# The last stage of a graph network: residual sum by accumulating transposes, deeper buffers, later steps

## The reference, cut to what matters

```python
alpha = ex / (denom[dst] + 1e-16)                    # softmax over the edges of one node, 4 heads
agg = segment_sum(vj * alpha[:, :, None], dst)       # 128 channels a node
out = agg.reshape(n, HID) + (x @ Wskip + bskip)
h = gelu(gelu(out @ W1 + b1) @ W2 + b2)
x = layernorm(x + (out + h))                         # no scale, no shift
```

## Time and profile before

| | |
|---|---|
| time, median of 3 runs (lowest, highest) | 7416.07 us (7416.06, 7416.97) |
| span of the profiled execution | 7463.9 us |
| busy in the span: TensorE, VectorE, GpSimd, ScalarE | 6262.2, 6114.0, 4840.9, 3838.3 us |
| last stage: first block's transpose to last scatter | 6651.07 to 7456.24 us |

### The profile page before, as it was taken

How to read it: one execution, slowest core, us unless ns; L and a number is a source line. 1 busy time by engine, 2 the same in 40 slices (tenths; PEclk the granted TensorE clock), 3 DMA queues, 4 the chain that set the end, 5 groups by cost and what they waited for, 6 DMA issues and landing times. The chain is left out here.

```text
span 7463.9 us, 156875 instructions
## 1 busy us (share of the span) xinstructions
PE 6262.2 (84%) x37260; PEld 5197.7 (70%) x37260; DVE 6114.0 (82%) x15796; ACT 3838.3 (51%) x10696; POOL 4840.9 (65%) x5469
## 2 busy tenths in 40 slices
PE   7699889899999657989989998999888765877776
PEld 3588888888889436867766676667666554865664
DVE  8588778787888777889879977997799887878887
ACT  6466666666666576733661166116622233654443
POOL 0488888888873576855776577657744565546665
PEclk8799999999999899999999999999999998988998
DMA  0365555554444466879779977997799765543432
GB/s 2 102 165 161 161 160 158 162 161 152 146 145 152 146 190 199 247 257 297 229 223 332 329 226 224 331 327 228 230 385 387 259 186 151 152 138 119 125 123 86
DMA packets 981268, 1483.74 MB, mean 199 GB/s; under 512 B 156967, under 2 KB 450705, under 8 KB 980647
## 3 DMA queue, kind: packets, MB, share of 16 engines
q1 hardware_dynamic: 685479, 922.39, 37.2%
q0 software_dynamic: 141504, 309.42, 16.2%
q10 hardware_dynamic: 153664, 244.12, 9.0%
HBM read 902.58 MB, written 573.11 MB: 198 GB/s over the span
## 5 line engine op out<-in xcount | busy, mean ns | idle before, releaser
L1336 PE MATMUL bank<-c_rows,sums_all 128*128 128x256 f32 (+1 forms) x3920 | 1320.9, 420 | 550.5 <-DVE c_rows L1487 304.3
L751 PE MATMUL bank<-wf_w,c_xt 128*128 128x256 f32 x6272 | 1615.0, 381 | 2.0 <-DVE y L1545 2.0
L1381 ACT ACTIVATE c_xt<-bank 128x512 f32<-128x512 f32 (+1 forms) x980 | 556.8, 568 | 1586.6 <-issue 831.0
L1307 POOL DMA_INDIRECT c_rows<-t_tab,src_pair x784 | 870.2, 1110 | 705.6 <-PE bank L1336 546.2
L1336 PEld LDWEIGHTS bank<-c_rows,sums_all 128*128 128x128 f32 x3920 | 633.9, 194 | 984.7 <-DVE c_rows L1487 478.7
L751 PEld LDWEIGHTS bank<-wf_w,c_xt 128*128 128x128 f32 x6272 | 1133.7, 191 | 127.0 <-ACT c_xt L1381 3.5
L1487 DVE SCALAR_TENSOR_TENSOR c_rows<-bank,carry,c_rows 32x256 f32<-32x256 f32 (+1 forms) x1950 | 913.7, 469 | 274.3 <-PE bank L1336 117.6
L1307 POOL DMA_INDIRECT c_rows<-z_tab,src_pair x784 | 770.7, 983 | 293.3 <-issue 189.5
L1085 DVE TENSOR_TENSOR lx_lo<-bank,lx_hi 128x512 fp32r<-128x512 f32 (+1 forms) x1000 | 658.6, 659 | 260.6 <-ACT lx_hi L1030 217.4
L1030 ACT ACTIVATE lx_hi<-bank 128x512 fp32r<-128x512 f32 (+1 forms) x1000 | 569.4, 572 | 580.4 <-PE bank L999 418.6
L741 PE MATMUL bank<-wf_hi,lx_hi 128*128 128x256 f32 x3200 | 725.0, 309 | 62.7 <-issue 49.4
(11 more groups left out here) (333 smaller groups left out, 14629.2 us busy)
## 6 DMA issues: line engine op xcount, KB each, us to landing
c_z<-z_tab SPq DMA_DIRECT2D x882, 256.0 KB
z_tab<-lz SPq DMA_DIRECT2D x400, 256.0 KB
t_tab<-lt SPq DMA_DIRECT2D x400, 256.0 KB
z_tab<-y ACTq DMA_DIRECT2D x392, 256.0 KB
c_own<-z_tab SPq DMA_DIRECT2D x392, 256.0 KB
t_tab<-y ACTq DMA_DIRECT2D x392, 256.0 KB
c_own<-t_tab SPq DMA_DIRECT2D x392, 256.0 KB
fl_x<-x_tab SPq DMA_DIRECT2D x396, 128.0 KB
```

Source lines behind the costliest of these rows:

```text
L751: last = nc.tensor.matmul(out, x(k), w[:, k, :], start=(k == 0), stop=(k == ks - 1 and not bias))
L1307: pool.indirect_dma_start(out=rows[:, s, i, 0:win], out_offset=None, in_=source, in_offset=bass.IndirectOffsetOnAxis(ap=m["src_i"][:, t:t ...
L1336: nc.tensor.matmul(psum[s % 2][:, i * win:(i + 1) * win], sums[:, j * 2 + i, :], rows[:, s, i, 0:win], start=True, stop=True).then_inc(S[" ...
L1381: nc.scalar.activation(xt[:, s % 2].rearrange("p k n -> p (k n)")[:, 0:n], psum[2 + s % 2][:, 0:n], ACT.Copy).then_inc(S["copied"], 1)
```

## The change

The second load of x and VectorE's two additions go. `back` no longer transposes one finished sum: it transposes `xt`, `skip` and `down` of a half block one after the other into the same PSUM bank, accumulating (six transposes a block where there were two). ScalarE copies the result to `y` (`result`), where VectorE had written it. The `agg` product with the identity is marked as a transpose. `xt`, `skip` and `y` get 6 slots, the statistics 8, and the scatters count on a ring of 6. `back` runs 4 turns after its block's first (before 5), the moments 5 (6), `scale_both` 8 (7), `scatter_both` 9 (7). `divide` and `norm` are cut into single steps that are interleaved in VectorE's list.

```diff
-                            "down_set": 1, "sum": 1, "back": 1, ...
+    out_ring = counts.phase(finish, {"scattered*": 32}, ring=6)
-        x_again = sb("fl_x2", [P, 4, 2, D])
-        xt = sb("fl_xt", [P, 2, 2 * P])
-        skip = sb("fl_skip", [P, 4, 2 * P])
+        xt = sb("fl_xt", [P, 6, 2 * P])
+        skip = sb("fl_skip", [P, 6, 2 * P])
-        both = sb("fl_sum", [P, 2, 2 * P])
-        y = sb("fl_y", [P, 4, 2, D])
+        y = sb("fl_y", [P, 6, 2, D])
# SyncE
-                                 (BEGIN - 4, every, load), (5, each, far_again)])
+                                 (BEGIN - 4, every, load)])
# GpSimd
-                in_turns(total, [(7, each, scatter_both), (6, each, invert)])
+                in_turns(total, [(9, each, scatter_both), (6, each, invert)])
# TensorE
                         for i in range(2):
                             last = nc.tensor.matmul(psum[3][:, i * P:(i + 1) * P], agg[:, c % 4, i, :], ident[:],
-                                                    start=False, stop=(i == 1))
+                                                    start=False, stop=(i == 1), is_transpose=True)
                 def back(j):
-                    pe.wait_ge(S["sum"], fp.at("sum", j))
+                    pe.wait_ge(S["down_set"], fp.at("down_set", j))
                     if j >= 2:
                         pe.wait_ge(S["y"], fp.at("y", j - 2))
                     for i in range(2):
-                        last = nc.tensor.transpose(psum[6 + j % 2][:, i * P:(i + 1) * P],
-                                                   both[:, j % 2, i * P:(i + 1) * P], ident[:])
+                        half_ = psum[6 + j % 2][:, i * P:(i + 1) * P]
+                        terms = (xt[:, j % 6, :], skip[:, j % 6, :], down[:, j % 2, :])
+                        for n, term in enumerate(terms):
+                            last = nc.tensor.matmul(half_, term[:, i * P:(i + 1) * P], ident[:], start=(n == 0),
+                                                    stop=(n == 2), is_transpose=True)
-                                 (BEGIN + 3, every, add_up(1)), (2, each, up_), (3, each, down_), (5, each, back)])
+                                 (BEGIN + 3, every, add_up(1)), (2, each, up_), (3, each, down_), (4, each, back)])
# ScalarE
+                def result(j):
+                    act.wait_ge(S["back"], fp.at("back", j))
+                    if j >= 6:
+                        act.wait_ge(S[f"scattered{j % 6}"], out_ring.ring_at("scattered", j, j % 6, back=1))
+                    nc.scalar.activation(y[:, j % 6, :, :].rearrange("p i c -> p (i c)"), psum[6 + j % 2][:, 0:2 * P],
+                                         ACT.Copy).then_inc(S["y"], 1)
-                in_turns(total, [(0, each, copy), (1, 1, line_copy), ...
+                in_turns(total, [(5, each, result), (0, each, copy), (1, 1, line_copy), ...
# VectorE
-                                 (BEGIN + 2, every, carry_on(0)), (7, each, scale_both),
-                                 (BEGIN + 5, every, divide), (6, each, norm), (BEGIN + 3, every, carry_on(1)),
-                                 (4, each, add), (BEGIN + 1, every, weigh)])
+                                 (BEGIN + 2, every, carry_on(0)), (BEGIN + 5, every, denominators),
+                                 (5, each, moments), (BEGIN + 5, every, inverses), (5, each, aggregate),
+                                 (BEGIN + 5, every, of_leads), (8, each, scale_both), (5, each, variance),
+                                 (BEGIN + 3, every, carry_on(1)), (BEGIN + 5, every, divide),
+                                 (BEGIN + 1, every, weigh)])
```

More of the change, by code:

```diff
@@ L124, in ring_at @@
         rate = self.rate[name + "*"]
-        return (j - s) * (rate // self.ring) + (self.base.get(name + str(s), 0) + rate * (1 - back))
+        before = (j - s) // self.ring * rate if isinstance(j, int) else (j - s) * (rate // self.ring)
+        return before + (self.base.get(name + str(s), 0) + rate * (1 - back))
     def end(self, name):
@@ L2174, in down_ @@
                     if j >= 2:
-                        act.wait_ge(S["sum"], fp.at("sum", j - 2))
+                        act.wait_ge(S["back"], fp.at("back", j - 2))
                     nc.scalar.activation(down[:, j % 2, :], psum[5][:, 0:2 * P], ACT.Gelu_apprx_tanh,
                                          bias=m["b_down"][:]).then_inc(S["down_set"], 1)
-                in_turns(total, [(0, each, copy), (1, 1, line_copy), (1, each, skip_), (2, each, up_), (3, each, down_),
+                def result(j):
+                    act.wait_ge(S["back"], fp.at("back", j))
+                    if j >= 6:
+                        act.wait_ge(S[f"scattered{j % 6}"], out_ring.ring_at("scattered", j, j % 6, back=1))
+                    nc.scalar.activation(y[:, j % 6, :, :].rearrange("p i c -> p (i c)"), psum[6 + j % 2][:, 0:2 * P],
+                                         ACT.Copy).then_inc(S["y"], 1)
+                in_turns(total, [(5, each, result), (0, each, copy), (1, 1, line_copy), (1, each, skip_), (2, each, up_), (3, each, down_),
                                  (18, 1, weight)])
@@ L2299, in carry_on, with denominators, inverses, of_leads @@
                     return step
[L2301 removed]
+                def denominators(j):
                     s = j % 4
                     dve.wait_ge(S["summed"], ph.at("summed", j))
[L2304 to L2305 removed]
                     bank = psum[s % 2][:, 0:2 * wide].rearrange("p (i n) -> p i n", i=2)
                     v.tensor_scalar(den[:, s, :, :], bank[:, :, D:wide], DEN_EPS, None, ALU.add).then_inc(S["den"], 1)
+                def inverses(j):
+                    s = j % 4
                     dve.wait_ge(S["den"], ph.at("den", j, 1))
                     v.reciprocal(den[:, s, :, :], den[:, s, :, :]).then_inc(S["den"], 1)
+                def of_leads(j):
+                    s = j % 4
                     dve.wait_ge(S["den"], ph.at("den", j, 2))
@@ L2313, in divide @@
                                     ALU.mult).then_inc(S["den"], 1)
+                def divide(j):
+                    s = j % 4
+                    if j >= 4:
+                        dve.wait_ge(S["skip"], fp.at("skip", order.index(j - 4)))
+                    bank = psum[s % 2][:, 0:2 * wide].rearrange("p (i n) -> p i n", i=2)
                     dve.wait_ge(S["den"], ph.at("den", j, 3))
@@ L2319, in divide, with moments, aggregate @@
                     last.then_inc(S["shared"], 1)
[L2321 to L2324, removed]
-                    v.tensor_tensor(both[:, j % 2, :], skip[:, j % 4, :], down[:, j % 2, :], ALU.add
-                                    ).then_inc(S["sum"], 1)
-                def norm(j):
-                    s = j % 4
-                    dve.wait_ge(S["back"], fp.at("back", j))
-                    dve.wait_ge(S[f"others_in{s}"], fp.ring_at("others_in", j, s))
-                    if j >= 4:
-                        dve.wait_ge(S[f"scattered{s}"], fp.ring_at("scattered", j, s, back=1))
-                    v.tensor_tensor(y[:, s, :, :].rearrange("p i c -> p (i c)"), psum[6 + s % 2][:, 0:2 * P],
-                                    x_again[:, s, :, :].rearrange("p i c -> p (i c)"), ALU.add).then_inc(S["y"], 1)
+                def moments(j):
+                    s = j % 8
                     dve.wait_ge(S["y"], fp.at("y", j))
                     for i in range(2):
-                        last = v.bn_stats(stats[:, s, i, :], y[:, s, i, :])
+                        last = v.bn_stats(stats[:, s, i, :], y[:, j % 6, i, :])
                     last.then_inc(S["stats"], 1)
+                def aggregate(j):
+                    s = j % 8
                     dve.wait_ge(S["stats"], fp.at("stats", j, 1))
```

53 lines of the change are left out of this document (24 added, 29 removed).

## The result

The kernel after the change took 7437.79 us (median; 7430.23 to 7444.59) beside 7417.19 for the kernel before in the same sessions (7411.68 to 7424.34). The ratio is 1.0027, with an interval of 1.0019 to 1.0034: 20.6 us or 0.27% slower. The forecast was 7421, with a range of 7365 to 7455, so the time lies inside the range, and 17 us above the forecast. The direction was given as even between faster and the same, with slower the least likely of the three; the change is slower by a little more than the 0.2% that can be told from nothing.

What follows compares the result with a forecast made beforehand. Bound before: power, scale, scatter at 7.40 us a round; after: a ring through TensorE at 7.34. Terms -5 + 34 - 5 - 13 - 6 + 0 = +5 on 7416 gave 7421 us, range 7365 to 7455.

Steps and rivals of the forecast that it cites:

- the slots: `result` waits for the scatter of six blocks earlier: 4.96 + landing L, 6.5 us, under 7.34, so no cost.
- the head: Last stage up to its first `carry_on(1)`: GpSimd's two turns go from 7.4 to 6.3 us; -6 us, bounds 0 and -9.
- the part with one block a round: 19 rounds after the steady part, forecast to go from 5.74 to 5.0 us each: -13 us.
- the ring through TensorE: Steady part: `add_up(1)`, `back`, `result`, moments, scaling, `carry_on(1)` become the bound at 7.34 us a round, 7.2 to 7.9.
- Full-clock rounds: The 78 steady rounds at full clock go from 7.40 to 7.34 us each: -5 us.
- The clock's falls: Steady part: TensorE's drops to 1.2 GHz now cost 1.7 us each; 20 taken, +34 us, bounds 0 and 58.
- the clock stays up: Rival: TensorE's stop of 2.0 us is too short for a clock drop, total 7387 us; chance 0.20.
- the single long rounds: 8.5 us of few long steady rounds; those from GpSimd meet 1.1 us of slack: -5 us.
- Drain: Last four pairs of blocks, where power and scatter still follow each other at 7.40 us: change 0.
- GpSimd's ring: Rival: GpSimd's own work bounds the steady part at 6.28 us a round, total 7310 us; chance 0.11.
- Scaling stretches the scatters: Rival: VectorE's scaling keeps GpSimd from writing descriptors, GpSimd needs 7.40 us a round, total 7397 us; chance 0.08.
- Slower: the falls all come: Rival: 34 clock drops in the longer ring, or a landing of 2.8 us, total 7445 us; chance 0.16.

Runs made afterwards that it cites:

- scale_even: Kernel after with `scale_both` at start 7 instead of 8, so it falls in even turns of the steady part: 7333.94 us, ratio 0.9884.
- warm_filler: Kernel after with three matmuls a round, result never read, on TensorE ahead of `add_up(1)`: 7404.91 us, ratio 0.9978.
- y_eight: Kernel after with 8 slots of `y` and scatters counted on a ring of 8, `xt` and `skip` with 5 slots: 7414.44 us, ratio 0.9994.
- before_decoupled: Kernel before with `scatter_both` at start 9 instead of 7, `y` with 6 slots, statistics with 8: 7368.95 us, ratio 0.9936.

## Why the prediction came out as it did

The time came out within the range, at +20.6 where +5 had been added up. The ring that bounds the kernel and the price of a fall were right. The step that failed is the one on the slots, and the terms of the head and of the part with one block a round were too favourable.

**The bound: right.** "the ring through TensorE becomes the bound at almost the old period, and GpSimd's 6.28 stays unused" is what the chain of after shows, and `scale_even` shows that what holds GpSimd's 6.28 back is the scaling in that ring. Its terms were forecast at 4.44 + 0.04 + 0.38 + 0.04 + 2.02 + 0.42 = 7.34. The chain has 0.42 for carry to `add_up(1)`, 4.42 for TensorE (6990.19 to 6994.61), 0.44 for `result` with its handovers, and 1.96 from the moments to the carry (6995.05 to 6997.01): 7.24. The moments to the carry had been put at 2.02. The accumulating transposes cost what the passes of `agg` in the earlier trace rows had said: six starts between 6951.56 and 6952.11, 0.11 apart. VectorE's short steps hid where they were said to hide.

```profile
6951.56 0.27 PE L2127 MATMUL bank<-ident,fl_xt 128*128 128x128 f32 x1
6951.68 0.27 PE L2127 MATMUL bank<-ident,fl_skip 128*128 128x128 f32 x1
6951.78 0.27 PE L2127 MATMUL bank<-ident,fl_down 128*128 128x128 f32 x1
...
6952.11 0.27 PE L2127 MATMUL bank<-ident,fl_down 128*128 128x128 f32 x1
```

**Full-clock rounds:** forecast 78 x (7.34 - 7.40) = -5, measured 78 x (7.24 - 7.40) = -12.5. The ring was 0.10 shorter than its sum.

**The clock's falls:** the mechanism and the price were right (1.67 each, forecast 1.7), the number was 25, not 20, and so +42 instead of +34. The kernel before had 33 rounds with a fall, where the prediction had worked out some 34. The open question was whether a stop of 2.0 still lets the clock fall: it does, in 16 of the 67 rounds that have such a stop. The other 9 falls come behind stops of 2.24 to 3.40, which late landings made and which the prediction did not have. So 20 was nearer to the truth than it looks, partly by luck: it was a choice between 0 and 34, and no row had told it. The rival "the clock stays up" gave 7387, and `warm_filler`, whose clock did stay up, has 7405: 33 to 35 us less than after and not the 40 of 24 falls fewer, because the stray rounds grew by 5. The prediction also says that it needs more than 29 falls to be slower by over 0.2%; its own sum reaches +15 with 26 (+5, and 6 falls more at 1.7).

**The slots, and the single long rounds:** this is the step that failed. The prediction has "6.5, under 7.34, so it costs nothing" for the slots and "Of the 8.5 us, those from GpSimd now meet 1.1 us of slack: -5" for the long rounds. Those of GpSimd went (`y_eight` has none between 7.3 and 8.7), and others came in their place, 9.6 us over 7.24, so +1 instead of -5. They come from the slots, for the landing L, counted from the end of the issue, was taken as one number, 1.57, from a gather's consumer in the earlier trace rows. The threshold was right: 4.96 + L against 7.24 decides from L = 2.3 on. But L is a distribution. Its median is 1.2, even shorter than assumed; `result` waits 17 times in 78 rounds, and in the round at 6997.01 L is up to 3.8. `y_eight` takes the wait away, and the stray rounds and eight falls with it: the term was worth 23 us by the medians and had been put at 0.

**One block a round:** forecast -13 (its own product, 19 x (5.0 - 5.74), is -14), measured -7.4. The rounds alternate between 5.05 and 5.29 (forecast 5.0), which is 3 of the 6.7 missing. The first two take 6.99 and 6.18, and one further on 5.96. These three, and no other of the 19, have a granted clock of 0.71 to 0.76: falls, which the prediction had not put into this part. They are the rest.

**Head:** forecast -6, measured +0.9. From the second power on GpSimd takes 10.9, 8.7, 7.7, 6.9, 6.5 and 6.2 from one power to the next, so its ring of 6.3 is reached only where the head ends. The first power comes 24.9 us into the head, before 22.6. Beside VectorE's long scans over the running maximum a scatter takes longer:

```profile
6633.02 1.85 DVE L2251 TENSOR_TENSOR_SCAN r_up_to<-r_starts,r_side,r_al 128x784 f32<-128x784 f32 x1
6633.21 2.52 POOL L2031 DMA_INDIRECT out_dram<-fl_y,node_of  x1 [2.98 <-DVE fl_y L2362]
```

The head before had that too (its power beside the same scan took 2.52), so this alone doesn't explain the miss. The slots cost here as well: `result` waits 8.2 us for landings in the head, in 5 waits, and `y_eight` has a head of 75.4, 3.0 less. How the rest of the 7 us divides was not tried.

**Drain:** forecast 0, measured +0.2.

The sum of the terms is then -12.5 + 42 + 1 - 7.4 + 0.9 + 0.2 = +24.2 on the profiled execution, +20.6 by the medians. Against the forecast of +5 the stray rounds are off by 6, the head by 7, the part with one block by 6, the falls by 8, and the ring by -7.5 on the other side. The landing stands behind three of these at once, the stray rounds, the falls and a part of the head, and without it the change would have been neutral. That the total was only 17 us off is in part luck, for the ring's error ran the other way.

**The rivals.** GpSimd's ring (7310, given 0.11) did not come by itself and came with one digit changed. "Scaling stretches the scatters" (0.08) is refuted for this kernel: in `scale_even` the scatter beside the scaling took 0.97 and the scaling 1.21 instead of 1.12. The Trainium skill (SBUF — State Buffer, section "SBUF: two separate sides") says that VectorE in a two-port mode, or with two SBUF inputs against a GpSimd operation that reads SBUF, and GpSimd exclude each other for a whole instruction. In which mode the scaling ran no run here shows; the trace shows no such lock for it, and agrees with the rule beside the scan, which has two tensor inputs, where the scatter took 2.52. "Slower: the falls all come" had the side right and the cause half: 25 falls and not 34, with the landing added. It also said that a landing of 2.8 would do as much, for every round; it took only the 17 waits.

## What to carry to other kernels

Before work is moved off the engine with the highest busy share, write out the rings, step by step, with every instruction that stands in the queue between two of their steps: the change took 153 us of work from VectorE and made one ring longer by the same edit, and where it put a 1.1 us step (in the odd or in the even turn) was worth 104 us, four times the 25 us of the transposed sum with all that came along with it. A ring that passes through a queue twice has two ways through it, and a step is out of the ring only if it is out of both. Give a buffer slots for the longest landing and not for the usual one: the wait came 17 times in 78 rounds, the median hid it, and it was the difference between a change that does nothing and one that costs 0.3%. And when a round waits for one thing, look at what the engines do in the next: here the longer stop was mostly followed by a lower clock.

## What the runs showed of the hardware

- TensorE's granted clock falls to its lower level (1.2 GHz) in 16 of 67 rounds with stops of 1.95 to 2.2 us, and in 9 of 11 with stops of 2.24 to 3.40 (the kernel after); each fall makes the round 1.67 us longer. In one of them TensorE stood for 1.97 ahead of 6957.83, and at 6959.22 its transposes were 0.21 apart instead of 0.11. With stops of mostly 1.00 (`scale_even`) 3 of 78 rounds have a fall and the clock is 0.99; with three matmuls put into the stop (`warm_filler`) it is one round and 1.00. In `before_decoupled`, with stops of 1.4 in the mean, it is 5 rounds and 0.98.
- A scatter's time from the start of its instruction to its landing has a median of 2.2 us. Among those for which the profile has a landing the longest is 3.3 in the steady part; the one at 6998.52 took up to 4.8, by the wait that it ended.
- Scaling on VectorE (128x128, float32, one tensor operand) leaves a scatter on GpSimd at 0.97; beside a scan of 128x784 it takes 2.5.
- A transpose that accumulates into a bank costs the same 0.11 us from start to start as one that doesn't, at full clock.
